# Issuing the next step's attention scores ahead of the last transposes and value products in the 16-head stage of a two-layer decoder

## Chip, core and metric

The kernel runs on one core of one Trainium2 chip. The metric is the device time of one launch in microseconds (us). Engines are PE (TensorE matmul; its weight loads are listed apart as PEld), DVE (VectorE), ACT (ScalarE), POOL (GpSimd) and SP, which issues DMAs.

## The reference

A two-layer decoder over x of shape (4, 512, 256), all in float32. Each sublayer is added to x and followed by a layer norm:

```python
x = _layernorm(x + _L0_attn_ref(...))    # one head, rotary
x = _layernorm(x + _L0_xattn_ref(...))   # one head, over ctx
x = _layernorm(x + _L0_ffn_ref(...))     # 8 experts, top 2
x = _layernorm(x + _L1_attn_ref(...))    # 16 heads of 16, causal
x = _layernorm(x + _L1_xattn_ref(...))   # 16 heads of 16, over ctx, with a mask
x = _layernorm(x + _L1_ffn_ref(...))     # 6 layers of local attention and MLP
```

The change is in the stage that computes the fourth and fifth line. For one of them and one batch entry:

```python
q, k, v = heads(x @ Wq.T), heads(src @ Wk.T), heads(src @ Wv.T)
scores = q @ k.T / sqrt(16)         # per head 512 x 512
scores = where(masked, -1e9, scores)
out = softmax(scores) @ v           # then merged heads @ Wo.T
```

## The kernel before

The whole decoder is one program of consecutive stages (`stage_wide`, `stage_moe`, `stage_heads`, `stage_l1_ffn`). `stage_heads` is the one touched. It walks eight bodies: four batch entries of the causal self-attention, then four of the cross-attention. A body has 16 steps n; step n is the query tile t = n // 4 (128 rows) and the head group g = n % 4 (four heads). In causal bodies a step looks at (t + 1) * 128 keys, in cross bodies always at 512.

The order of the work is written out by hand in `body()`, a generator that yields named steps. Each engine walks the same list and executes only the kinds that belong to it, so an engine's instruction stream is its own kinds in list order, and the engines meet at semaphores. Nothing reorders the list. The kinds that matter here:

- `s` (PE, L1962): the scores of one step, four heads side by side on 32 rows each, into PSUM banks 4 to 7. Before the first of them PE waits until all four banks have been emptied, which means for the fourth `max` of the step before.
- `max` (DVE, L2136, one per head): scores plus mask from PSUM into `h_prob`, with the row maximum. After the fourth comes `h_nb` (L2141), the scaled negative maximum.
- `e` (ACT, L2059, one per head): the exponential, in place in `h_prob`, of the step before (e = n - 1).
- `pt` (PE, L1972, one per head, here called passes 0 to 3): transposes of `h_prob` of two steps before (m = n - 2), one 128x128 block per 128 keys, into banks 2 and 3 in turn. The copies to `h_pT` (L2027) are ACT's for passes 0 and 2, DVE's for 1 and 3.
- `pv` (PE, L1994): the value products of step n - 3, 16 small matmuls per 512 keys, accumulating in bank 1.
- `first` and `second`, lists of extra work of some steps: the projections for the next body `q` (n = 1, 9), `k` (n = 2, 6, 10, 14) and `v` (n = 4, 12), the row sums `den` and the division `div` (n % 4 = 3), the output projection `wo` (n % 4 = 0), the transposes of x `xt` (n = 0). `rs` (DVE, n % 4 = 1) inverts the row sums, `ln` (n = 5) and `norm` (n = 6) are the layer norm, `mask` (n % 4 = 1) turns a tile of the integer mask into numbers.

Of the kernel before, what the change touches and what calls it, by code (L numbers as in the profile page):

```python
# [1715 lines left out]
def stage_heads(nc, shared, w_self, w_cross, preload):  # L1716
# [11 lines left out]
    N = TB * QC  # L1728
# [3 lines left out]
    with ExitStack() as ctx:  # L1732
# [41 lines left out]
        def body():  # L1774

            def of(m):  # L1780
                return -1 if m < 0 else 0

            units = {1: ("q", 0), 2: ("k", 0), 6: ("k", 1), 9: ("q", 1), 10: ("k", 2), 14: ("k", 3)}
            for n in range(N):
                e, m = n - 1, n - 2
                first, second = [], []
                if n in units:
                    first.append((units[n][0], 1, units[n][1]))
                if n % 4 == 3:
                    t = (n - 7) // 4  # L1790
                    first += [("den", of(t), t % TB), ("div", of(t), t % TB)]
                if n % 4 == 0:
                    t = (n - 8) // 4
                    first.append(("wo", of(t), t % TB))
                if n == 0:
                    first += [("xt", 1, 0), ("xt", 1, 1)]
                if n in (4, 12):
                    second.append(("v", 1, n // 8))
                yield ("s", 0, n)
                if n % 4 == 1:  # L1800
                    t = (n - 5) // 4
                    yield ("rs", of(t), t % TB)
                yield from [("max", 0, n, 0), ("max", 0, n, 1), ("pt", of(m), m, 0), ("e", of(e), e, 0),
                            ("e", of(e), e, 1), ("pt", of(m), m, 1), *first, ("max", 0, n, 2), ("max", 0, n, 3),
                            ("pt", of(m), m, 2), ("e", of(e), e, 2), ("e", of(e), e, 3), ("pt", of(m), m, 3), *second]
                if n == 5:
                    yield ("ln", -1)
                if n == 6:
                    yield from [("norm", -1), ("bo", 1)]
                if n % 4 == 1:  # L1810
                    yield ("mask", 0, TB - 1) if n == 1 else ("mask", 1, n // 4 - 1)
                yield ("pv", of(n - 3), n - 3)

        full = list(body())
        banks, ring = {}, 0
        for step in full:
# [644 lines left out]
```

## Time and profile before

| | |
|---|---|
| median of 3 runs | 4191.61 us (4185.91 to 4193.18) |
| profiled execution | 4192.44 us, span 4190.6 us |
| busy share of the span | PE 93%, PEld 61%, DVE 69%, ACT 62%, POOL 30% |
| mean granted TensorE clock | 0.974 |
| `stage_heads` in the trace | scores from 558.9 us on, last transposes about 1223 us |

The profile is of one execution. Busy shares are averages over all stages. Times in the trace count from the start of the span, so the execution's own time is 1.8 us above the span, and 0.8 us above the median of the runs.

### The profile page before, as it was taken

The numbers are of one execution on the slowest core, as the hardware profiler recorded it, in microseconds if no ns is written. First come the engines' busy times: TensorE is split into PE (matmuls) and PEld (weight loads), VectorE is DVE, ScalarE is ACT, GpSimd is POOL, SyncE is SP. The second block draws the span as 40 slices with busy tenths as digits, with TensorE's granted clock in tenths as the row PEclk, the third lists the DMA queues.
The fourth block names the chain that finished last, engine by engine and source line by source line (L and its number), as shares of the span: only waits on it lengthen the run. The fifth ranks groups of instructions, "written<-read, shape, count | busy, mean of one in ns | idle before, by whom it ended". The sixth has DMA issues, their size and how long they took to land.

```text
span 4190.6 us, 85556 instructions
## 1 busy us (share of the span) xinstructions
PE 3887.8 (93%) x30488; PEld 2558.7 (61%) x30488; DVE 2907.0 (69%) x10276; ACT 2577.9 (62%) x6856; POOL 1243.1 (30%) x810
## 2 busy tenths in 40 slices
PE   8979478899988999999999999999999999999986
PEld 5668445566655666666666666666666666666664
DVE  3542357788868877777777777777777777777773
ACT  2213146677756767667676676676766766767662
POOL 1103300000005443433343434333434343334330
PEclk9979789999999999999999999999999999999998
DMA  6002210000010001110010101110011101111010
GB/s 180 23 20 74 66 59 2 7 24 17 9 52 19 22 22 47 31 40 19 17 51 27 42 16 53 29 33 23 23 46 31 37 21 41 29 39 29 16 36 18
DMA packets 110881, 145.54 MB, mean 35 GB/s; under 512 B 36020, under 2 KB 77344, under 8 KB 110080
## 3 DMA queue, kind: packets, MB, share of 16 engines
q1 hardware_dynamic: 107056, 130.76, 11.0%
q0 software_dynamic: 3408, 9.31, 0.8%
q8 instruction: 251, 4.11, 0.4%
q14 instruction: 166, 1.36, 0.1%
HBM read 78.31 MB, written 11.40 MB: 21 GB/s over the span
## 4 chain that ended last, share of the span: by engine, by line
PE 55%; DVE 9%; POOL 4%; issue 2%; DMA 1%; ACT 0%; SPq 0%; DVEq 0%; POOLq 0%
PE psum L496 18%; PE psum L591 9%; PE psum L476 7%; PE psum L575 6%; PE psum L608 5%; PE psum L554 4%; PE psum L529 4%; POOL f_rn L898 3%; DVE f_rot L716 2%; DVE f_rot L718 1%; DVE f_ss L723 1%; DVE f_xn L813 1%; DVE f_prob L759 1%; PE psum L597 1%; DVE f_prob L787 1%
## 5 line engine op out<-in xcount | busy, mean ns | idle before, releaser
L496 PE MATMUL psum<-f_wqkv,f_xsT 128*128 128x512 f32 x2304 | 1076.4, 595 | 4.3 <-ACT f_raw L641 2.7
L893 POOL TENSOR_TENSOR f_raw<-f_rot 128x512 f32<-128x512 f32 x384 | 488.2, 1271 | 1689.8 <-DVE f_rot L718 1689.8
L655 ACT ACTIVATE f_prob<-f_prob,f_nb,f_rq 128x128 f32<-128x128 f32 x1536 | 740.1, 488 | 37.2 <-DVE f_nb L772 36.3
L496 PEld LDWEIGHTS psum<-f_wqkv,f_xsT 128*128 128x128 f32 x2304 | 400.8, 191 | 322.9 <-issue 318.3
L898 POOL TENSOR_TENSOR f_rn<-f_ss,f_half_pow 128x32 f32<-128x32 f32 x96 | 523.1, 5449 | 11.3
L759 DVE CUSTOM_DVE_ANT_0 f_prob<-psum,f_band 128x128 f32<-128x128 f32 x1536 | 352.7, 284 | 130.6 <-PE psum L529 129.2
L591 PE MATMUL psum<-f_xnT,f_w 128*128 128x512 f32 x960 | 437.5, 595 | 2.2 <-ACT f_hT L678 1.1
L639 ACT ACTIVATE f_sq<-psum 128x512 f32<-128x512 f32 x384 | 227.5, 593 | 229.2 <-PE psum L496 229.1
L787 DVE TENSOR_SCALAR f_prob<-f_prob,f_rs 128x128 f32<-128x128 f32 x1536 | 343.3, 287 | 13.5
L575 PE MATMUL psum<-f_wo,f_oT 128*128 128x256 f32 x1536 | 347.4, 379 | 1.6 <-ACT f_v L641 0.9
L716 DVE TENSOR_TENSOR f_rot<-f_raw,f_tab 128x512 f32<-128x512 f32 x384 | 332.8, 867 | 16.0 <-DMA x_before_mlp<-x_all 16.0
L575 PEld LDWEIGHTS psum<-f_wo,f_oT 128*128 128x128 f32 x1536 | 289.8, 190 | 71.3 <-issue 35.7
L2059 ACT ACTIVATE h_prob<-h_prob,h_nb 128x512 f32<-128x512 f32 (+3 forms) x512 | 324.7, 639 | 0.0
L591 PEld LDWEIGHTS psum<-f_xnT,f_w 128*128 128x128 f32 x960 | 179.0, 191 | 209.8 <-issue 200.9
L655 ACT ACTIVATION_READ_ACCUMULATOR f_prob<-f_prob,f_nb,f_rq 128x1 f32 x1536 | 295.4, 192 | 0.0
L666 ACT COPY f_oT<-psum 128x512 f32<-128x512 f32 x192 | 111.5, 580 | 284.9 <-PE psum L554 284.9
L1972 PEld LDWEIGHTS psum<-ident,h_prob 128*128 128x128 f32 x1664 | 181.9, 141 | 154.6 <-ACT h_prob L2059 77.4
L1972 PE MATMUL psum<-ident,h_prob 128*128 128x128 f32 x1664 | 246.9, 279 | 30.0 <-DVE h_pT L2027 16.0
L688 DVE COPY f_pT<-psum 128x512 f32<-128x512 f32 x192 | 131.8, 687 | 192.0 <-PE psum L476 192.0
L718 DVE TENSOR_TENSOR f_rot<-f_raw,f_tab 128x512 f32<-128x512 f32 x384 | 262.3, 683 | 0.0
L723 DVE TENSOR_REDUCE f_ss<-f_sq 128x8 f32<-128x512 f32 x384 | 259.8, 676 | 0.0
L476 PEld LDWEIGHTS psum<-ident,f_raw 128*128 128x128 f32 x1536 | 185.9, 141 | 108.2 <-issue 100.7
(249 smaller groups left out, 7069.6 us busy)
## 6 DMA issues: line engine op xcount, KB each, us to landing
f_v_near<-f_v SPq DMA_DIRECT2D x168, 256.0 KB, 3.4
f_wqkv<-in_Wqkv SPq DMA_DIRECT2D x36, 512.0 KB, 5.8
w_moe_W<-in_L_ffn_W SPq DMA_DIRECT2D x2, 4096.0 KB, 23.1
f_w<-in_W SPq DMA_DIRECT2D x12, 640.0 KB
f_wo<-in_Wo SPq DMA_DIRECT2D x6, 1024.0 KB, 6.4
f_xs<-x_all SPq DMA_DIRECT2D x24, 254.0 KB
expert_rows<-m_y SPq DMA_DIRECT2D x39, 128.0 KB, 1.7
h_mask_int<-in_mask_BxSxS_ik SPq DMA_DIRECT2D x16, 256.0 KB, 2.6
```

The lines of the kernel that those rows point to most:

```text
L476: mm = nc.tensor.transpose(ps.ap(key)[:, slot * P:(slot + 1) * P], src, ident[:])
L496: mm = nc.tensor.matmul(ps.ap(step), xsT[:, c, t * P:(t + 1) * P], wqkv[:, c, i * HALF:(i + 1) * HALF], start=c == 0, stop=c == KC - 1)
L575: mm = nc.tensor.matmul(ps.ap(step)[:, 0:D], oT[:, c, :], wo[:, c, :], start=c == 0, stop=c == OC - 1)
L591: mm = nc.tensor.matmul(ps.ap(step), w1[:, c, at:at + P], xnT[:, c, :], start=c == 0, stop=c == KC - 1)
L655: ex = nc.scalar.activation(pr, pr, ACT.Exp, bias=nb[:, t % 2, h:h + 1], scale=rq8[:, t, h:h + 1], accum_out=sums[:, t % 2, h:h + 1])
L716: nc.vector.tensor_tensor(heads(rot[:, n % 2, 0, :]), heads(q), cos, ALU.mult)
L759: red = nc.vector.tensor_tensor_reduce(prob[:, (4 * n + 2 * j + i) % 16, :], ps.ap(key)[:, (n % 2 * 2 + j) * P:(n % 2 * 2 + j + 1) * P], b ...
L787: ins = nc.vector.tensor_scalar(pr, pr, rs[:, t % 2, h:h + 1], None, ALU.mult)
L893: nc.gpsimd.tensor_tensor(raw[:, (4 * t + i) % 8, :], rot[:, n % 2, 0, :], rot[:, n % 2, 1, :], ALU.add).then_inc(rope_done, 1)
L898: nc.gpsimd.tensor_tensor(rn[:, t % 2, :], ss[:, t % 2, :], half_pow[:], ALU.pow).then_inc(rn_ready, 1)
L1972: mm = nc.tensor.transpose(ps.ap(step)[:, k * P:(k + 1) * P], prob[:, n % 3 * HPC + i, k * P:(k + 1) * P], ident[:])
L2059: nc.scalar.activation(pr, pr, ACT.Exp, bias=nb[:, t % 2, h:h + 1], scale=scale, accum_out=sums[:, t % 2, h:h + 1]).then_inc(exp_ready, 1)
```

## The change

In `body()` the step's scores are no longer its first item. Step 0 keeps its scores at the front. In every step n below 15 the scores of step n + 1 are issued between the exponentials and pass 3 of the transposes. The `second` list and `pv` follow pass 3 as they did.

```diff
@@ -1796,13 +1796,15 @@
                     first += [("xt", 1, 0), ("xt", 1, 1)]
                 if n in (4, 12):
                     second.append(("v", 1, n // 8))
-                yield ("s", 0, n)
+                if n == 0:
+                    yield ("s", 0, n)
+                early = [("s", 0, n + 1)] if n + 1 < N else []
                 if n % 4 == 1:
                     t = (n - 5) // 4
                     yield ("rs", of(t), t % TB)
                 yield from [("max", 0, n, 0), ("max", 0, n, 1), ("pt", of(m), m, 0), ("e", of(e), e, 0),
                             ("e", of(e), e, 1), ("pt", of(m), m, 1), *first, ("max", 0, n, 2), ("max", 0, n, 3),
-                            ("pt", of(m), m, 2), ("e", of(e), e, 2), ("e", of(e), e, 3), ("pt", of(m), m, 3), *second]
+                            ("pt", of(m), m, 2), ("e", of(e), e, 2), ("e", of(e), e, 3), *early, ("pt", of(m), m, 3), *second]
```

Only PE executes `s`, so only PE's stream changes; those of DVE, ACT, POOL and SP hold the same instructions in the same order as before. Two places of PE's stream in the first cross body follow. L1962 of the kernel before is L1964 of the changed one, and so on by two lines. Of L1972 (L1974), x4 is one pass of transposes, x8 two, x16 four.

The first place is PE's steps 2 and 3 in the kernel before: passes 0 and 1, the keys' projection, passes 2 and 3, value products, then the scores of step 3.

```order
970 L1972 MATMUL psum<-ident,h_prob 128x128 x8
971 L1938 MATMUL psum<-h_srcT,w_x1_Wk 128x512 x2
972 L1972 MATMUL psum<-ident,h_prob 128x128 x8
973 L1994 MATMUL psum<-h_pT,h_v 32x128 x16
974 L1962 MATMUL psum<-h_kT,h_qT 128x512 x4
975 L1972 MATMUL psum<-ident,h_prob 128x128 x8
976 L2007 MATMUL psum<-ident,h_rs_wide 128x128 x2
```

The same place on PE in the changed kernel:

```order
1029 L1974 MATMUL psum<-ident,h_prob 128x128 x8
1030 L1940 MATMUL psum<-h_srcT,w_x1_Wk 128x512 x2
1031 L1974 MATMUL psum<-ident,h_prob 128x128 x4
1032 L1964 MATMUL psum<-h_kT,h_qT 128x512 x4
1033 L1974 MATMUL psum<-ident,h_prob 128x128 x4
1034 L1996 MATMUL psum<-h_pT,h_v 32x128 x16
1035 L1974 MATMUL psum<-ident,h_prob 128x128 x8
1036 L2009 MATMUL psum<-ident,h_rs_wide 128x128 x2
```

Pass 3 and the value products now stand between the scores and the next pass 0; before, they stood ahead of the scores.

The second place is PE's steps 4 and 5 in the kernel before, with the output projection (`Wo`) and the values' projection (`Wv`):

```order
980 L1972 MATMUL psum<-ident,h_prob 128x128 x8
981 L2018 MATMUL psum<-w_a1_Wo,h_oT 128x256 x2
982 L1972 MATMUL psum<-ident,h_prob 128x128 x8
983 L1950 MATMUL psum<-w_x1_Wv,h_srcT 128x256 x4
984 L1994 MATMUL psum<-h_pT,h_v 32x128 x16
985 L1962 MATMUL psum<-h_kT,h_qT 128x512 x4
986 L1972 MATMUL psum<-ident,h_prob 128x128 x16
```

The same place on PE in the changed kernel:

```order
1041 L1974 MATMUL psum<-ident,h_prob 128x128 x8
1042 L2020 MATMUL psum<-w_a1_Wo,h_oT 128x256 x2
1043 L1974 MATMUL psum<-ident,h_prob 128x128 x4
1044 L1964 MATMUL psum<-h_kT,h_qT 128x512 x4
1045 L1974 MATMUL psum<-ident,h_prob 128x128 x4
1046 L1952 MATMUL psum<-w_x1_Wv,h_srcT 128x256 x4
1047 L1996 MATMUL psum<-h_pT,h_v 32x128 x16
1048 L1974 MATMUL psum<-ident,h_prob 128x128 x12
```

The values' projection, too, moved from ahead of the scores to behind them.

## Rows read from the trace of the kernel before

**Rows 1.** The page: span, and busy time of each engine with its share.

```profile
span 4190.6 us, 85556 instructions
...
PE 3887.8 (93%) x30488; PEld 2558.7 (61%) x30488; DVE 2907.0 (69%) x10276; ACT 2577.9 (62%) x6856; POOL 1243.1 (30%) x810
```

**Rows 2.** Cross bodies: length; busy PE, PEld, DVE, ACT, POOL; granted clock; DMA.

```profile
852.00:1221.00 369.00, 337.76 (x3910) 228.68 (x3903) 301.27 (x861) 265.49 (x677) 11.47 (x7) 1.00 0.04 12
```

**Rows 3.** Waits, 559 to 1221 us: waiter, awaited, us in all, times, longest.

```profile
DVE h_prob L2136 <- PE psum L1962: 65.9, 94, 1.5
```

**Rows 4.** Timeline of a cross step 8: start, duration, engine, work [idle before].

```profile
993.37 1.14 PE L1962 MATMUL psum<-h_kT,h_qT 32*128 32x512 f32 x8 [0.35 <-DVE h_mx L2136]
994.44 1.09 PE L1972 MATMUL psum<-ident,h_prob 128*128 128x128 f32 x8
994.64 0.69 DVE L2136 CUSTOM_DVE_ANT_0 h_prob<-psum,h_add_mask 128x512 f32<-128x512 f32 x1 [0.62 <-PE psum L1962]
995.13 0.58 ACT L2027 COPY h_pT<-psum 128x512 f32<-128x512 f32 x1 [1.74 <-PE psum L1972]
...
995.37 1.03 PE L2018 MATMUL psum<-w_x_Wo,h_oT 128*128 128x256 f32 x4
...
997.25 1.08 PE L1994 MATMUL psum<-h_pT,h_v 128*32 128x128 f32 x32
...
998.18 0.17 DVE L2141 TENSOR_SCALAR h_nb<-h_mx 128x4 f32<-128x4 f32 x1
...
998.29 1.14 PE L1962 MATMUL psum<-h_kT,h_qT 32*128 32x512 f32 x8
```

**Rows 5.** Timeline of a cross step 15, with the row sums and the division.

```profile
1034.56 1.09 PE L1972 MATMUL psum<-ident,h_prob 128*128 128x128 f32 x8
...
1037.60 0.42 DVE L2165 TENSOR_TENSOR h_oT<-h_o_raw,psum 128x256 f32<-128x256 f32 x1 [0.96 <-ACT h_o_raw L2074]
...
1039.39 1.14 PE L1962 MATMUL psum<-h_kT,h_qT 32*128 32x512 f32 x8 [0.74 <-DVE h_mx L2136]
1040.46 0.77 PE L1972 MATMUL psum<-ident,h_prob 128*128 128x128 f32 x5
```

**Rows 6.** Timeline of a cross step 10, with a keys' projection.

```profile
1005.99 1.88 PE L1938 MATMUL psum<-h_srcT,w_x_Wk 128*128 128x512 f32 x4
...
1007.91 0.75 DVE L2093 TENSOR_SCALAR h_kT<-psum,w_x_bk 128x512 f32<-128x512 f32 x1 [0.74 <-PE psum L1938]
...
1009.91 0.17 DVE L2141 TENSOR_SCALAR h_nb<-h_mx 128x4 f32<-128x4 f32 x1
```

**Rows 7.** Timeline of a cross step 12, the values' projection.

```profile
1019.72 1.89 PE L1950 MATMUL psum<-w_x_Wv,h_srcT 128*128 128x256 f32 x8
...
1021.65 0.76 DVE L2106 TENSOR_TENSOR h_v<-psum,w_x_bv 128x256 f32<-128x256 f32 x2 [0.20 <-PE psum L1950]
```

**Rows 8.** Timeline: layer norm statistics and mask; then `rs` and a plain step.

```profile
981.28 1.39 DVE L2176 BATCH_NORM_STATS2 h_stat<-x_all 128x6 f32<-128x256 f32 x4
...
983.21 0.42 DVE L2115 TENSOR_SCALAR h_add_mask<-h_mask_int 128x512 f32<-128x512 int32 x1
...
1046.47 0.25 DVE L2150 RECIPROCAL h_rs<-h_sums 128x16 f32<-128x16 f32 x1 [0.85 <-ACT h_prob L2059]
...
1047.10 0.69 DVE L2136 CUSTOM_DVE_ANT_0 h_prob<-psum,h_add_mask 128x512 f32<-128x512 f32 x1
...
1050.26 0.17 DVE L2141 TENSOR_SCALAR h_nb<-h_mx 128x4 f32<-128x4 f32 x1
```

**Rows 9.** Timeline: starts of like scores, a causal body apart, and cross.

```profile
700.52 0.50 PE L1962 MATMUL psum<-h_kT,h_qT 32*128 32x128 f32 x8 [0.74 <-DVE h_mx L2136]
...
775.49 0.50 PE L1962 MATMUL psum<-h_kT,h_qT 32*128 32x128 f32 x8 [0.74 <-DVE h_mx L2136]
...
1087.29 1.14 PE L1962 MATMUL psum<-h_kT,h_qT 32*128 32x512 f32 x8 [0.35 <-DVE h_mx L2136]
```

**Rows 10.** Timeline of PE in the next stage, four transposes behind a wait.

```profile
1291.40 1.12 PE L476 MATMUL psum<-ident,f_prob 128*128 128x128 f32 x4 [2.66 <-DVE f_prob L787]
```

## The prediction, made before the changed kernel ran

> **What bounds the stage now.** The page comes first: PE is busy 3887.8 of 4190.6 us [rows 1], and the cross bodies of the stage look alike, PE 337.76 of 369 us (92%), DVE 82%, ACT 72%, granted clock 1.00 [rows 2]. That invites the reading "PE is full, and DVE waits for it", and the waits seem to say so: DVE stands still 65.9 us in 94 waits for the scores [rows 3]. It is what the change is aimed at. But the timeline of one step shows a ring of two engines. In step 8 the scores start at 993.37, the first `max` at 994.64, 1.27 later; `h_nb` follows the fourth `max` at 998.18, and the next scores start at 998.29, 0.11 behind it [rows 4]. The scores of step n + 1 need all four banks of step n empty, so they cannot start before the fourth `max` is done, wherever they stand in the list. In the row-sum steps PE even stood idle for it, 0.74 us ahead of the scores at 1039.39 [rows 5]. Most steps end this way, DVE's last `max` releasing the scores.
>
> While DVE works through the `max` operations, PE does passes 0 to 3 and the value products. That work is cover: it is done before the scores are allowed, or nearly so. The reader should see in [rows 4] that pass 0 starts at 994.44 and the value products at 997.25, all inside the time that DVE needs anyway.
>
> **What the change does to this ring.** It puts scores(n + 1), which must wait for DVE's fourth `max`, in front of pass 3 and the value products, which need not wait for it. PE takes its stream in order, so pass 3, the values' projection where there is one, and the value products now start only after that wait. Nothing is added or removed: 120 of 128 score groups move, the DMAs don't, SP's and POOL's queues are not passed. DVE's own order is unchanged: after `h_nb` it must copy pass 3 to `h_pT` before it may take the next `max`. So DVE now waits for scores and then pass 3 before it can go on.
>
> *The start of a step, counted from the scores' start.* Scores hold PE for 1.07 (993.37 to 994.44), a pass 0.54 (two in 1.09), and the copy starts 0.69 after its pass began (994.44 to 995.13) [rows 4]. Pass 3 starts at 1.07, DVE copies it at 1.76 and, one wide operation taking 0.61 from start to start, reaches the first `max` at 2.37 instead of 1.27. The value products take 1.04 (997.25 to 998.29) [rows 4], so pass 0 starts at 1.07 + 0.54 + 1.04 = 2.65 instead of 1.07.
>
> *The rest of the step.* From the first `max` to `h_nb` a step with nothing extra on DVE takes 3.16 (1047.10 to 1050.26) [rows 8], with 0.11 to the next scores 3.27. That gives the new intervals from one scores' start to the next in a cross body (512 keys):
>
> - n = 1, 9: `rs` ahead of the first `max` costs 0.63 (1046.47 to 1047.10) [rows 8]: 2.37 + 0.63 + 3.27 = 6.27.
> - n = 2, 10, 14: the keys' projection starts after passes 0 and 1, at 2.65 + 1.0 = 3.65; DVE takes it 1.92 later and is at `h_nb` 2.00 after that [rows 6]: 3.65 + 1.92 + 2.00 + 0.11 = 7.7.
> - n = 3, 7, 11, 15: pass 0 leads over ACT's copy, two exponentials and the copy of the output to the division and on to the scores in 4.83 (1034.56 to 1039.39) [rows 5]: 2.65 + 4.83 = 7.48.
> - n = 4, 8, 12: from the start of the output projection to the next scores 2.92 (995.37 to 998.29) [rows 4]: 3.6 + 2.92 = 6.5.
> - n = 5, 13: the values' projection now lies behind the scores and pass 3. It starts at 1.61, DVE copies it 1.93 later [rows 7], in 0.76, then `rs` 0.63 and 3.27: 8.2.
> - n = 6: the layer norm statistics take DVE 1.93 (981.28 to 983.21), the mask about 0.35 [rows 8], the keys' copy 0.7, since PE is done by then: 2.37 + 1.93 + 0.35 + 3.27 + 0.7 = 8.6.
> - n = 0: its scores stay where they were, and scores(1) no longer stand behind pass 3 and value products: 1.27 + 3.27 + 0.35 for the output projection's addition = 4.9.
>
> Sum: 4.9 + 12.5 + 23.1 + 29.9 + 19.5 + 16.4 + 8.6 = 114.9. A cross body takes 93.92 now (993.37 to 1087.29) [rows 4, 9]: +21.0. Three bodies are like this. The last cross body has no projections to hide behind; its plain steps go from about 4.9 to about 6, and I count it as the same 21. Together +84.
>
> *Causal bodies.* The same steps with 128, 256, 384 and 512 keys. Scores, passes, copies, `max` and value products shrink with the keys (scores 0.50 at 128 [rows 9], 1.14 at 512 [rows 4]), the projections don't. Walking the 16 steps in the same way gives 4.3, 5.2, 5.4, 4.3 (128 keys), 3.7, 5.7, 5.7, 5.3 (256), 4.8, 4.7, 6.2, 6.0 (384), 5.9, 7.8, 7.2, 7.2 (512), together 89.4, against 74.97 now (700.52 to 775.49) [rows 9]: +14.4. The first body starts with an empty pipeline, about 2 less: 4 x 14.4 - 2 = +56.
>
> *The clock.* PE will now idle between pass 2 and the scores: in a row-sum step pass 2 ends near 4.6 and the scores come at 7.48, 2.8 us idle, and about as much in step 6. Today's stage has a granted clock of 1.00 [rows 2] and no such gap. In the next stage a gap of 2.66 us stands ahead of four transposes that took 1.12 [rows 10], against 0.54 for a pass here: PE had fallen from its higher level (2.4 GHz) to its lower one (1.2 GHz). Bounds: no fall costs 0. A fall after each of the about 20 gaps of that size (4 in each cross body, 1 in each causal) costs the scores' 1.07 and the pass's 0.54 once more, 1.6 each, +32; with the gaps of about 2 us taken in as well, another 16 at 1.6, +58. I take half of the 32, since one row shows a fall and none shows that it always comes.
>
> **Sum.** 84 + 56 + 16 = +156 on the profiled execution's own 4192.4, which is 0.8 above the median of the runs: 4347.5 in median terms.
>
> **A rule weighed against the rows.** At 1039.39 PE stood idle for 0.74 us at scores that waited for `max`, with transposes behind them that started only at 1040.46, after the scores [rows 5]; nothing behind the waiting instruction was taken first. The Trainium skill, page "TensorE: Matmul & The Clock Gate", section "The mechanism" (of packing small matmuls), says that matmuls start and end in program order and that only weight loads are pulled ahead. By that rule the wait holds everything behind it; the trace agrees. The page "Perfetto Trace Analysis", section "Optimization Strategy", advises to find the gaps of the most used engine and to make what they wait for start sooner. By that rule the change should pay, and DVE's 65.9 us [rows 3] would be its upper bound, 4126; it is the gain rival below, and the trace speaks against it, since what releases the scores is not PE's position but DVE's last `max`.
>
> **Rivals.**
>
> - *The scores gain.* Where PE is late rather than DVE, the scores start sooner. Most of DVE's waits for them go, up to 65.9 us: 4126. For it: PE is busy 92% here [rows 2], and in steps with a projection behind pass 1 or pass 3 it may come late to the scores. It decides if the copy of pass 3 does not lie on DVE's way to the next `max`. But the list has it there, so only steps 0, 4 and 12 can gain, and 5 and 13 give back more. 3%.
> - *Nothing changes.* PE passes the waiting scores, or the delay hides under DVE's extras: 4192. [Rows 5] speak against it. 2%.
> - *Half the size.* DVE's 1.1 us later start per step is there, but the chain over pass 0 and the keys' projection has slack that my fixed distances don't see, since DVE then finds its inputs ready. 120 moved groups at 1.1 (2.37 less 1.27) are +132; with half of it hidden +66 are left: about 4258, and up to 4305 with a small share hidden. 8%.
> - *The clock falls often.* If the gaps near 2 us count too and a fall lasts over more than one scores' group: +140 + 58 and up, 4395 to 4450. 8%.
>
> **How the numbers follow.** The forecast has 79%: 4347, with no clock term 4331, and 15% off the serial term 4310; with the clock's +58 it is 4390. The range is 4308 to 4395, which leaves out about 2 in 10. A measurement of this kernel can tell about 0.2% (8 us) from no change. Slower: forecast, half size and clock, 95%. Same 2%, faster 3%.
>
> **What the changed profile would show.** In a cross body, 115 us from scores to the same scores of the next (93.9 now); the next scores 0.11 behind `h_nb` in nearly all moved steps; pass 3 at 1.07 behind the scores' start and DVE's copy of it waiting for PE, about 1.7 us per step, where today DVE waits for the scores; the waits of DVE for pass 3 above 150 us in all, and PE waiting for `max` 100 to 200 us; the step of the division near 7.5 and those behind the values' projection near 8.2. PE's busy share in the stage near 75%, and granted clock a little under 1.00. The forecast is wrong if DVE's copy of pass 3 finds its bank filled at once, if the interval of the steps 5 and 13 is not above 7, or if the later stages change.

## The result, and the profile after

| | before | changed |
|---|---|---|
| median, range | 4188.76 us (4185.21 to 4193.18, 4 runs) | 4372.32 us (4368.49 to 4377.75, 4 runs) |
| profiled span | 4190.6 us | 4375.9 us |
| mean granted clock | 0.974 | 0.961 |

The ratio is 1.0432, 95% interval 1.0416 to 1.0448: 183.6 us slower. The forecast was 4347 in a range of 4308 to 4395. From here on "scores at x" means the start of the score matmuls.

The page of the changed kernel: span, busy time of each engine, and, in 40 slices of the span, PE's busy share and granted clock in tenths.

```profile
span 4375.9 us, 85556 instructions
...
PE 3946.8 (90%) x30488; PEld 2587.9 (59%) x30488; DVE 2914.0 (67%) x10276; ACT 2578.3 (59%) x6856; POOL 1242.7 (28%) x810
...
PE   8979377777777899999999999999999999999997
...
PEclk9979689999998999999999999999999999999998
```

The number of instructions is the same as in [rows 1]; DVE has 2914 us of work against 2907, PE 3947 against 3888, which is the same work at a lower clock in places. Nothing was added. The span is longer by 185 us, and PE's share is down to 7 tenths in slices 6 to 13, the 16-head stage.

The waits in that stage (559 to 1400 us): waiter, awaited, us in all, times, longest.

```profile
DVE h_pT L2029 <- PE psum L1974: 224.3, 148, 3.1
...
PE psum L1964 <- DVE h_mx L2138: 177.4, 116, 2.8
...
DVE h_prob L2138 <- PE psum L1964: 5.1, 7, 1.5
```

The same two groups in the kernel before, 559 to 1221 us:

```profile
PE psum L1962 <- DVE h_mx L2136: 29.9, 58, 1.1
...
DVE h_pT L2027 <- PE psum L1972: 13.8, 20, 1.5
```

DVE's wait for the scores, 65.9 us in [rows 3], is down to 5.1. That is what the change aims at, and it arrived. But the wait did not go away, it moved one instruction ahead in DVE's order: DVE now waits 224.3 us at its copies of the transposes (13.8 before), some 202 of them for pass 3 and the rest for pass 1. PE waits 177.4 us (29.9 before) for DVE's last `max`, with pass 3 and the value products behind it.

The timeline of step 11 of the second cross body, from its scores to the next:

```profile
1130.52 1.14 PE L1964 MATMUL psum<-h_kT,h_qT 32*128 32x512 f32 x8 [1.72 <-DVE h_mx L2138]
...
1131.59 0.66 PE L1974 MATMUL psum<-ident,h_prob 128*128 128x128 f32 x4
1132.18 1.08 PE L1996 MATMUL psum<-h_pT,h_v 128*32 128x128 f32 x32
1132.29 0.69 DVE L2029 COPY h_pT<-psum 128x512 f32<-128x512 f32 x1 [1.71 <-PE psum L1974]
1132.89 0.68 DVE L2138 CUSTOM_DVE_ANT_0 h_prob<-psum,h_add_mask 128x512 f32<-128x512 f32 x1
1133.19 1.09 PE L1974 MATMUL psum<-ident,h_prob 128*128 128x128 f32 x8
...
1136.23 0.42 DVE L2167 TENSOR_TENSOR h_oT<-h_o_raw,psum 128x256 f32<-128x256 f32 x1 [1.22 <-ACT h_o_raw L2076]
...
1138.02 1.14 PE L1964 MATMUL psum<-h_kT,h_qT 32*128 32x512 f32 x8 [2.78 <-DVE h_mx L2138]
```

Read against [rows 4, 5]: pass 3 starts 1.07 behind the scores, DVE copies it at 1.77 after 1.71 us of waiting, and its first `max` is at 2.37 instead of 1.27. Pass 0 is at 2.67 instead of 1.07; from there to the next scores it is 4.83 us, exactly as in [rows 5]. The step takes 7.50 us instead of 5.90, and PE stands idle for 2.78 us at its end.

All 16 intervals of a cross body, from the starts of the scores in the traces (before: the body of [rows 4]; changed: the second cross body; the last row is that of experiment e3 below):

| step | 0 | 1, 9 | 2, 10, 14 | 3, 11, 15 | 4, 12 | 5, 13 | 6 | 7 | 8 |
|---|---|---|---|---|---|---|---|---|---|
| before | 6.44 | 5.70 | 6.04 | 5.90 | 6.63 | 4.90 | 6.40 | 5.90 | 4.92 |
| forecast | 4.9 | 6.27 | 7.7 | 7.48 | 6.5 | 8.2 | 8.6 | 7.48 | 6.5 |
| changed | 4.94 | 6.13 | 7.63 | 7.50 | 6.46 | 7.92 | 8.56 | 9.00 | 8.08 |
| changed, PE kept busy | 4.94 | 6.13 | 7.64 | 7.50 | 6.45 | 7.92 | 8.56 | 7.50 | 6.52 |

Steps 7 and 8 of the changed kernel stand out in this body. Such long steps come at other places too, and not at the same ones in each body: steps 4 and 12 take 9.28 and 8.01 us in the first cross body, 8.02 each in the third. The timeline of PE around steps 7 and 8 of the second:

```profile
1096.44 0.60 PE L1974 MATMUL psum<-ident,h_prob 128*128 128x128 f32 x4
1099.68 2.09 PE L1964 MATMUL psum<-h_kT,h_qT 32*128 32x512 f32 x8 [2.64 <-DVE h_mx L2138]
1101.70 1.11 PE L1974 MATMUL psum<-ident,h_prob 128*128 128x128 f32 x4
...
1108.68 1.14 PE L1964 MATMUL psum<-h_kT,h_qT 32*128 32x512 f32 x8 [2.78 <-DVE h_mx L2138]
1109.75 1.09 PE L1974 MATMUL psum<-ident,h_prob 128*128 128x128 f32 x4
```

After an idle 2.64 us the scores take 2.09 us instead of 1.14, and pass 3 1.11 instead of 0.66: PE is at its lower level (1.2 GHz). After the idle 2.78 ahead of 1108.68 the scores run at the higher level (2.4 GHz) and the pass behind them at the lower one. After 2.78 ahead of 1138.02, above, nothing fell. The granted clock over the whole stage, from the windows of the changed kernel (columns as in [rows 2]):

```profile
559.00:1406.00 847.00, 653.92 (x6483) 422.33 (x6484) 523.47 (x1693) 462.20 (x1332) 16.83 (x11) 0.93 0.03 8
```

It is 0.93, against 1.00 in the cross bodies of [rows 2].

### The profile page after: what moved, and what is told of

Read it like the earlier page. It is cut to its first block, busy times and chain, and to the rows that moved or that the text cites. A ratio compares the mean times of both kernels' runs of the same rounds, so it can differ in the third digit from the quotient of the medians.

```text
span 4375.9 us, 85556 instructions
## 1 busy us (share of the span) xinstructions
PE 3946.8 (90%) x30488; PEld 2587.9 (59%) x30488; DVE 2914.0 (67%) x10276; ACT 2578.3 (59%) x6856; POOL 1242.7 (28%) x810
## 3 DMA queue, kind: packets, MB, share of 16 engines
q0 software_dynamic: 3408, 9.31, 0.8%
## 4 chain that ended last, share of the span: by engine, by line
PE 53%; DVE 8%; POOL 4%; issue 2%; DMA 1%; ACT 0%; SPq 0%; DVEq 0%; POOLq 0%
PE psum L496 17%; PE psum L591 9%; PE psum L476 7%; PE psum L575 6%; PE psum L608 4%; PE psum L554 4%; PE psum L529 4%; POOL f_rn L898 3%; DVE f_rot L716 2%; DVE f_rot L718 1%; DVE f_ss L723 1%; DVE f_xn L813 1%; DVE f_prob L759 1%; PE psum L597 1%; DVE f_prob L787 1%
## 5 line engine op out<-in xcount | busy, mean ns | idle before, releaser
L2029 ACT COPY h_pT<-psum 128x512 f32<-128x512 f32 (+3 forms) x256 | 128.8, 503 | 378.4 <-PE psum L1974 378.3
L2029 DVE COPY h_pT<-psum 128x512 f32<-128x512 f32 (+3 forms) x256 | 151.0, 590 | 228.7 <-PE psum L1974 226.4
L1964 PE MATMUL psum<-h_kT,h_qT 32*128 32x512 f32 (+3 forms) x1024 | 138.5, 609 | 178.3 <-DVE h_mx L2138 177.4
L1974 PEld LDWEIGHTS psum<-ident,h_prob 128*128 128x128 f32 x1664 | 195.5, 149 | 160.6 <-issue 104.9
L1974 PE MATMUL psum<-ident,h_prob 128*128 128x128 f32 x1664 | 278.7, 297 | 12.1 <-ACT h_pT L2029 7.9
```

Of the source, the lines that this page charges most:

```text
L1974: mm = nc.tensor.transpose(ps.ap(step)[:, k * P:(k + 1) * P], prob[:, n % 3 * HPC + i, k * P:(k + 1) * P], ident[:])
```

## The experiments

All were timed against the kernel before on the same chip, whose median was 4189.7 us beside e1 to e4, 4190.5 beside e5 to e8 and 4189.7 beside e9 and e10. Theory: the loss is two delays behind a wait that PE takes in order (pass 3 for DVE's copy, pass 0 for ACT's chain and the projections), and a clock that falls in PE's new gap. The rivals: DVE's copy of pass 3 alone; the value products alone; no clock term.

**e1_behind_pass3.** The scores go behind pass 3, still ahead of the second list and the value products.

```diff
-                            ("pt", of(m), m, 2), ("e", of(e), e, 2), ("e", of(e), e, 3), *early, ("pt", of(m), m, 3), *second]
+                            ("pt", of(m), m, 2), ("e", of(e), e, 2), ("e", of(e), e, 3), ("pt", of(m), m, 3), *early, *second]
```

> The next step's scores are issued behind pass 3 but still ahead of the second list and the value products. Theory A (two delays: DVE's copy of pass 3 waits for PE, and pass 0 starts 1.58 us later): here the first delay is gone and pass 0 starts at 1.07 + 1.04 = 2.11 us instead of 1.07 (2.65 in the changed kernel). Walking the steps as in the prediction gives about +12.7 us for each cross body and +8.5 for each causal one, +85 in all, and up to 15 for the clock: 4270 to 4290. Rival B (it is all DVE's copy of pass 3): no later than the kernel before, 4190 or less. Rival C (the value products do not matter but their place behind the wait costs as much as everything): 4370.

Measured 4291.17 us, ratio 1.0241 (1.022 to 1.0262): 101 slower than before, 81 faster than the changed kernel. In the second cross body step 3 takes 6.91 us and steps 2 and 10 about 7.04; the walk with pass 0 at 2.11 gives 6.94 and 7.1. DVE's wait at its copies is 69.6 us here, against 224.3, and only some 15 of them are for pass 3. So more than half of the loss stays when DVE's copy of pass 3 finds its bank filled, and rival B falls. The total is 1 us above the expected range; the granted clock over the stage is 0.97, so some falls are in it.

**e2_values_first.** As the changed kernel, but the value products go ahead of the early scores.

```diff
-                            ("pt", of(m), m, 2), ("e", of(e), e, 2), ("e", of(e), e, 3), *early, ("pt", of(m), m, 3), *second]
+                            ("pt", of(m), m, 2), ("e", of(e), e, 2), ("e", of(e), e, 3), ("pv", of(n - 3), n - 3), *early, ("pt", of(m), m, 3), *second]
...
-                yield ("pv", of(n - 3), n - 3)
```

> As the changed kernel, but the value products are issued ahead of the early scores, so only pass 3 and the second list stand behind them. Theory A: the first max stays at 2.37 us behind the scores, pass 0 moves from 2.65 to 1.61; the walk gives about +13.6 us for a cross body and +10 for a causal one, and PE's gap ahead of the scores shrinks below 2 us, so the granted clock is back near 1.00: 4275 to 4300. Rival B (only DVE's copy of pass 3 counts): as the changed kernel, about 4370.

Measured 4305.4 us, ratio 1.028 (1.026 to 1.03): 67 faster than the changed kernel, with only the value products taken out from behind the wait. That is 5 us beyond the expected range: the keys' steps took 7.10 where the walk gave 6.7, and the clock over the stage was 0.98, not 1.00. Neither delay is the whole: each of them, alone, leaves 101 to 116 us of the 184, falls of the clock included.

**e3_fill.** As the changed kernel, with transposes of the identity ahead of the early scores. They write to the bank that pass 3 overwrites.

```diff
-                            ("pt", of(m), m, 2), ("e", of(e), e, 2), ("e", of(e), e, 3), *early, ("pt", of(m), m, 3), *second]
+                            ("pt", of(m), m, 2), ("e", of(e), e, 2), ("e", of(e), e, 3), ("fill", of(m), m, n), *early, ("pt", of(m), m, 3), *second]
...
+                    elif kind == "fill":
+                        m, n = step[2:]
+                        count = 0 if it == BODIES or (n in (0, 1, 9) and it < BODIES - 1) else \
+                            14 if n % 4 == 3 or n == 6 or it == BODIES - 1 else 6
+                        at = ("pt", off, m, 3)
+                        if count and n < N - 1:
+                            empty(at, it)
+                            for _ in range(count):
+                                nc.tensor.transpose(ps.ap(at)[:, 0:P], ident[:], ident[:])
```

> As the changed kernel, with 6 or 14 transposes of the identity into the bank of pass 3 (which pass 3 overwrites) ahead of the early scores, so that PE is busy in most of the gap. They add nothing to the result. If the part of the loss that my fixed distances leave open (184 measured, about 137 by the steps without a slow clock) is the granted clock: 1.00 in the stage and about 47 us less than the changed kernel, 4325 plus or minus 10; step 7 of a cross body 7.5 instead of 9.0. If it is something else (ready signals, bank traffic, the list order of the layer norm): 4370 or more.

Measured 4334.52 us, ratio 1.034 (1.0323 to 1.0358): 38 us faster than the changed kernel, with more work on PE. The window over the stage of this kernel, and PE's timeline at steps 7 and 8:

```profile
559.00:1366.00 807.00, 711.02 (x7457) 494.47 (x7457) 523.98 (x1688) 464.18 (x1339) 16.93 (x11) 1.00 0.03 8
```

```profile
1071.72 1.75 PE L1985 MATMUL psum<-ident 128*128 128x128 f32 x14 [0.67 <-DVE h_pT L2038]
1073.69 1.14 PE L1964 MATMUL psum<-h_kT,h_qT 32*128 32x512 f32 x8 [0.22 <-DVE h_mx L2147]
...
1079.32 1.75 PE L1985 MATMUL psum<-ident 128*128 128x128 f32 x14 [0.91 <-DVE h_pT L2038]
1081.19 1.14 PE L1964 MATMUL psum<-h_kT,h_qT 32*128 32x512 f32 x8
```

The granted clock is 1.00, the scores take 1.14 each time, and steps 7 and 8 take 7.50 and 6.52. This shows that the long steps 7 and 8 were the clock. In the last body the filler runs past the last `max`, up to 0.4 us a step (6.50 instead of 6.13), so the clock's share is a little above 38: with that some 41.

**e4_swap_copies.** As the changed kernel, but ACT copies pass 3 and DVE pass 2.

```diff
-                    elif kind == "pt" and step[3] % 2 == 0:
+                    elif kind == "pt" and step[3] in (0, 3):
...
-                    elif kind == "pt" and step[3] % 2 == 1:
+                    elif kind == "pt" and step[3] in (1, 2):
```

> As the changed kernel, but ACT copies pass 3 and DVE pass 2, so DVE no longer stands at the copy of pass 3 ahead of its next max; it still waits until PE has read the probabilities of pass 3. Theory A with pass 0 as the delay that binds most steps (row sums, keys, output projection): only about 2 to 3 us less in a body, 4345 to 4360. Theory with DVE's copy as what binds: 0.6 us less in each moved step, 70 in all, 4300.

Measured 4367.98 us, ratio 1.0423 (1.0401 to 1.0446), not to be told from the changed kernel and 8 us above what was expected. In the second cross body the steps did as expected: 1 and 9 from 6.13 to 5.85, 6 from 8.56 to 7.63, the rest unchanged at 7.64, 7.50 and 7.93. But steps 4 and 12 of this body, 6.46 without a fall, took 9.31, and falls come at other places of the stage too (granted clock 0.92): the clock took most of the gain back, which the expectation had not counted. e10 takes the clock out.

**e10_swap_and_fill.** The edits of e3 and e4 together.

> The swap of the copies of passes 2 and 3 together with the filler transposes. The swap alone shortened step 9 from 6.1 to 5.9 us and step 6 from 8.6 to 7.6 but the clock took it back. With PE kept busy the gain should show: about 12 us below the kernel with the filler alone (4334.5), 4318 to 4328. If the swap gives nothing by itself: 4334.

Measured 4320.55 us, ratio 1.0311 (1.0294 to 1.0328): 14 us below e3, with steps 4 and 12 at 6.45 and a granted clock of 1.00 over the stage. So in the cross bodies the swap shortens only steps 1, 9 and 6 (in the last body 1, 5, 9, 13 and 6). It does not free DVE from pass 3, though. The first `max` of a step writes the buffer of `h_prob` that pass 3 reads, and waits until it has been read:

```profile
DVE h_prob L2147 <- PE psum L1974: 77.6, 85, 1.9
```

That is e10 from 559 to 1400 us. What e4 and e10 take off DVE's way is the copy, not the wait. That the other steps hang on pass 0 or on the projections follows from the walk, and e1 and e9 support it.

**e9_moved_output_copy_early.** The changed kernel, with ACT's copy `h_o_raw` ahead of the two exponentials in the row-sum steps: a kind of its own on ACT, ahead of them in the list.

```diff
+                raw = [("oraw", of((n - 7) // 4), (n - 7) // 4 % TB)] if n % 4 == 3 else []
-                yield from [("max", 0, n, 0), ("max", 0, n, 1), ("pt", of(m), m, 0), ("e", of(e), e, 0),
+                yield from [("max", 0, n, 0), ("max", 0, n, 1), ("pt", of(m), m, 0), *raw, ("e", of(e), e, 0),
...
-                    elif kind == "den":
+                    elif kind == "oraw":
```

> The changed kernel with ACT's copy of the output ahead of the two exponentials in the steps with n % 4 = 3. If in the changed kernel these steps (7.5 us) hang on pass 0, which stands behind pass 3 and the value products, and on ACT's chain behind it: they take about 6.3 us, 1.2 less in each wide one, some 28 in all, and PE's gap ahead of the scores shrinks from 2.8 to about 1.6 us, so the clock falls less often, another 20 to 30: 4305 to 4335. If the clock does not hang on that gap: 4340 to 4350.

Measured 4319.17 us, ratio 1.0314 (1.0296 to 1.0332), 53 us below the changed kernel and inside the expected range. In the second cross body steps 3 and 11 take 6.18 instead of 7.50, and the granted clock over the stage is 0.97 instead of 0.93.

**e6_output_copy_early.** The same edit on the kernel before: what the study found there besides.

> The kernel before, with ACT's copy of the output (h_o_raw) ahead of the two exponentials instead of behind them, in the steps with n % 4 = 3; nothing moves on PE or DVE. If the chain pass 0, copy, two exponentials, h_o_raw, division sets these steps (5.9 us against 4.9 of a step without it), each of 32 shrinks by about 1.0: 4155 to 4165. If DVE's or PE's own work sets them: 4189.

Measured 4164.64 us, ratio 0.9946 (0.9933 to 0.996), 26 us faster than before. The timeline of a cross step 11 of this kernel (its lines lie one below those of the kernel before):

```profile
993.49 1.09 PE L1973 MATMUL psum<-ident,h_prob 128*128 128x128 f32 x8
...
994.18 0.58 ACT L2028 COPY h_pT<-psum 128x512 f32<-128x512 f32 x1 [1.44 <-PE psum L1973]
...
994.66 0.38 ACT L2075 COPY h_o_raw<-psum 128x256 f32<-128x256 f32 x1
...
995.49 0.41 DVE L2166 TENSOR_TENSOR h_oT<-h_o_raw,psum 128x256 f32<-128x256 f32 x1
...
997.28 1.14 PE L1963 MATMUL psum<-h_kT,h_qT 32*128 32x512 f32 x8
```

The division comes 2.00 behind pass 0, not 3.04 as in [rows 5], and DVE does not wait for it; the next scores come 3.79 behind pass 0, not 4.83. Step 7 gained only 0.4 (5.48), since the layer norm lies ahead of it on DVE, and the narrow causal steps less than 1.0, so the total is 26 and not 32 times 1.0.

**e5_values_proj_later.** The kernel before, with the values' projection in the first list of steps 5 and 13.

```diff
-                if n in (4, 12):
-                    second.append(("v", 1, n // 8))
+                if n in (5, 13):
+                    first.append(("v", 1, n // 8))
```

> The kernel before, with the values' projection issued in the first list of steps 5 and 13 instead of the second list of steps 4 and 12. It then lies ahead of DVE's third max, where PE has time, and no longer between the last max of step 4 and the scores of step 5. By the walk through the steps: step 4 from 6.6 to 4.9 us, step 5 from 4.9 to about 6.1, 0.4 to 0.5 a pair: 5 to 8 us faster in all, 4181 to 4185. If PE's sum of work is all that counts: no change, 4189.

Measured 4189.4 us, ratio 0.9995 (0.9986 to 1.0004): no gain, against 5 to 8 us expected. In cross bodies steps 4 and 5 take 4.89 and 6.05, 0.6 less together, as expected; but step 6 rose from 6.40 to 6.75, and in a causal body steps 4 and 5 rose from 7.46 to 7.67 together. The expectation had counted neither.

**e7_both.** e5 and e6 in one.

> The two edits of e5 and e6 in one kernel. They touch different steps, so the sum if both hold: 4148 to 4160.

Measured 4163.86 us, ratio 0.9935 (0.9922 to 0.9949). That is e6 alone within the intervals, as e5 gives nothing. It lies 4 us above the expected range, which counted e5's share.

**e8_only_step1.** The changed kernel's move in step 0 alone.

```diff
-                if n == 0:
+                if n != 1:
                     yield ("s", 0, n)
-                early = [("s", 0, n + 1)] if n + 1 < N else []
+                early = [("s", 0, n + 1)] if n == 0 else []
```

> The changed kernel's move in step 0 alone: only scores(1) are issued ahead of pass 3 and the value products. It is the step in which PE, not DVE, was late (6.4 us, scores 1.7 behind h_nb). If the gain there (1.5 us) were kept: 8 times 1.5, 12 us faster, 4178. If PE only shifts its work into step 1, whose pass 0 then comes 1.6 later: no gain, 4187 to 4200.

Measured 4193.14 us, ratio 1.0007 (0.9998 to 1.0016): no gain. In a cross body step 0 falls from 6.44 to 4.94 and step 1 rises from 5.70 to 7.29, 12.14 before and 12.23 now. In the kernel before PE was late there rather than DVE (the scores start 1.67 behind `h_nb`), and the early scores only shift PE's work by a step. PE is late at other places too, 1.27 at the end of steps 1 and 9 and 1.86 at the end of steps 4 and 12; no run moved the scores at those alone.

## Why the prediction was right

The mechanism held, and so did the serial term. Of the 28 us between the forecast loss (156) and the measured one (184), nearly all is the clock term, which was too small.

- **The ring.** The prediction said that DVE's last `max` releases the scores wherever they stand. In the changed trace they start 0.11 behind `h_nb` in nearly every moved step. DVE's wait for them fell from 65.9 to 5.1 us and bought nothing. Shown by the trace.
- **The two delays.** First `max` at 2.37 (measured 2.37), pass 0 at 2.65 (2.67). e1 and e2 each take one out of the changed kernel and get 81 and 67 us back; neither alone explains the loss. Where both run at once, the later one counts, so their shares don't simply add up.
- **What the profile was to show.** From scores to scores of the next cross body 115 us (117.0 measured in the second, its clock falls included), DVE waiting above 150 us for pass 3 (some 202 of the 224.3), PE 100 to 200 us for `max` (177.4), PE's busy share in the stage near 75% (77%, 653.92 of 847). All came, but the granted clock, said to be a little under 1.00, was 0.93.
- **The walk.** The intervals forecast for a cross body sum to 114.9 us; e3, with the clock kept up, took 113.9 (scores at 1024.55 to those at 1138.48). The cross and causal terms, 84 + 56 = 140 us, compare with 145 us that e3 lost, of which some 3 are its filler's. Largest misses: steps 5 and 13 (8.2 for 7.92).
- **The clock.** The mechanism was right and the size was off: the term was 16 us, and e3 gives 38 to 41. The step that failed is "I take half of the 32", that is, a fall behind every second of about 20 gaps, at 1.6 us each. The number of gaps was right: in the changed trace 19 of the stage's score groups wait 2.4 us or more. But 15 of the 19 are followed by a step that is longer than in e3, by 1.4 to 2.9 us and not by 1.6, about 27 us in all. The profiled stage is longer than that of e3 by 42 us, and the rest, some 15, comes behind shorter gaps, which the forecast put at nothing and only its upper bound took in. Step 14 of the first causal body, for example, takes 10.17 us instead of 7.25 behind a gap of 1.88. So the rival "the clock falls often" was half right: some falls cost more than the scores and one pass that the 1.6 stands for, and steps 7 and 8 of the second and of the last cross body are long one behind the other. The upper bound of +58 held.
- **The rule on order.** By the Trainium skill, page "TensorE: Matmul & The Clock Gate", section "The mechanism", matmuls stay in program order, and the trace agrees: at 1138.02 PE waited 2.78 us with pass 3 behind, whose probabilities had been ready a step earlier.
- **The gain rival** needed the copy of pass 3 off DVE's way. e4 and e10 took the copy off it, and e10 is still 3.1% slower than before; but there the first `max` still waits for pass 3 itself. The stronger test is e1, in which DVE hardly waits for pass 3 and which is 2.4% slower: pass 0 is late. The prediction named only steps 0, 4 and 12 as those that can gain. In steps 1 and 9 PE came late too, and steps 1 and 2 together rose from 11.74 to 13.76 us all the same.
- **Half size** (4258 to 4305) fell: the slack that it supposed is not there, since each step ends on the chain that the delay hits.

Left open: why a gap of 2.78 us brought the clock down at one place and not at another in the same trace. No run varied the length of the gap by itself. Nor did any run take the values' projection alone out from behind the wait. Steps 5 and 13, the ones behind it, went from 4.90 to 7.92 us each, 6 of the 20 us of a cross body, and their price rests on the walk (8.2).

## What to carry to other kernels

By these runs an instruction that must wait for another engine is cheapest behind everything on its own engine that need not wait. Moving it forward to "start sooner" gains only if the thing it waits for is already there; otherwise all that it was moved past is late by the wait, and here a wait of 66 us on DVE went, while its waits for transposes rose from 14 to 224 us and PE's for DVE from 30 to 177. Before such a move, look at what released the instruction (here the last `max`, whose `h_nb` starts 0.11 us ahead of it), and then at the chain inside the step: here the gain was to be had on ACT, by a copy of 0.35 us that stood behind two exponentials.

## What the runs showed of the hardware

- Work without use can make a kernel faster: up to 14 transposes in the gap ahead of the scores gave 38 us back (e3), since the granted clock of the stage went from 0.93 to 1.00.
- Behind waits of 2.4 to 2.8 us a fall of the clock made a step longer by 1.5 to 1.6 us in most places and by up to 2.9 in others (step 4 of the first cross body 9.28 instead of 6.45; steps 4 and 12 of e4 9.31). Behind 4 of 19 such waits in the changed kernel the step was no longer than in e3. It is a cost that an edit elsewhere can trigger: the swap of e4 saved 14 us by the steps (e10 against e3) and lost about 10 of them to the clock.
